# Waiting for each group of four indirect transfers to land before the next group is issued, in a four-layer graph network

## The chip, the cores and the metric

The kernel runs on one core of one Trainium2 chip. The metric is the device time of one execution in microseconds (us), as the median of several runs. The engines are named as the profile names them: PE is TensorE, DVE is VectorE, ACT is ScalarE, POOL is GpSimd, SP is SyncE, which here issues the plain transfers.

## The reference

A graph of 6250 nodes and 100,000 edges, sorted by destination, with 128 features per node, goes through four layers. Each layer adds its result to the input and normalises the rows. Every layer works on rows gathered by edge:

```python
edge_index = jnp.stack([src, dst])
x = _layernorm(x + _L0_gnn_ref(x, edge_index, edge_weight, ...))       # three hops of a weighted sum over edges
x = _layernorm(x + _L1_gnn_ref(x, node_type_8, src, dst, edge_type_8, ...))  # typed attention, softmax over dst
x = _layernorm(x + _L2_gnn_ref(x, edge_index, ...))                    # attention on leaky_relu(x_l[src] + x_r[dst])
x = _layernorm(x + _L3_gnn_ref(x, edge_index, ...))                    # attention, softmax over src, summed over dst

def spmm(z):                                                           # one hop of layer 0
    return jax.ops.segment_sum(edge_weight[:, None] * z[col], row, num_segments=N)
```

## The kernel before

Edges are handled in chunks of 128, one edge per partition, and chunks in groups of four (`G = 4`). There are 784 chunks of edges (`EC`, 196 groups), or 832 (`CH`, 208 groups) where the list is padded so that each chunk touches one block of 128 nodes. Whatever is addressed by an edge's index goes through an indirect transfer that POOL issues: one instruction per chunk, 128 rows each, 7200 of them in all. The stages follow one another:

- `scatter_edges` (issue at L726, 784 transfers): DVE and PE work out the place of every edge in the order by source, and POOL scatters records of four numbers (16 bytes) to these places in HBM. POOL waits for `placed`, once per group.
- `hop`, called three times (issue at L1094, 784 transfers each): POOL gathers rows of 512 bytes into a ring of 16 groups, in `rows`. SP waits for each group's `got` and counts `landed`; PE multiplies the landed rows by weighted one-hot tiles (L1137); DVE makes these tiles (L1171) and adds the sums (L1184). From the 17th group on POOL waits for PE's count `summed` before it issues a group. Beside hops 1 and 2 the places for the order by destination are worked out, beside hop 0 a histogram.
- `scatter_ranked` (issue at L1292, 784 transfers): the scatter into the order by destination. POOL waits for nothing between its transfers. PE, DVE, ACT and SP go on to the dense work of layer 0 meanwhile.
- `softmax_pass`, called three times (issue at L1443; 832, 832 and 784 transfers): rows of 1024, 528 and 512 bytes are gathered for layers 1, 2 and 3. The ring is 11, 15 and 16 groups deep. Before it reuses a slot, POOL waits for DVE's `weighed` or `scored` (L1815, L1752).
- `weigh_and_sum` (issue at L1938, 832 transfers of 1056-byte rows): the change doesn't touch it.

Each group has a completion semaphore per ring slot (`got[s]`, `sent[s]`), raised by 16 by each transfer once it has landed, so 64 per group and turn of the ring. In `scatter_ranked` the four transfers of a group raise four different semaphores. POOL executes its instructions in the order in which they are written; the code isn't reordered by a scheduler.

Of the kernel before, what the change touches and what calls it, by code (L numbers as in the profile page):

```python
# [21 lines left out]
G = 4  # L22
SLOTS = 4
# [21 lines left out]
RING = 16  # L45
# [532 lines left out]
def scatter_edges(nc, k, rec, keys, first_place, table, name):  # L578


    with ExitStack() as ctx:
# [25 lines left out]
        sent = [sem(f"sent{s}") for s in range(SLOTS)]  # L607
# [4 lines left out]
        @block.scalar  # L612
        def _(act):
            def turn_onehots(n, b):

                act.wait_ge(turned_ok, n + 1)
                act.wait_ge(looked, n * G + G)
                nc.scalar.copy(oh_lo_t[:, b, :, :], turned[:, b, 0:G, :]).then_inc(lo_t, 1)

            def a_round(i, first):  # L620
                for s in range(SLOTS):
                    n = i * SLOTS + s
                    if not first:

                        act.wait_ge(sent[s], i * 64)
                    nc.scalar.copy(records[:, s, :, :], rec[:, bass.ds(i * SLOTS * G + s * G, G), :]).then_inc(taken, 1)
                    for g in range(G):
                        if g == G - 1:
                            turn_onehots(n + 1, (s + 1) % 2)

                        act.wait_ge(next_ready, n * G + g + 1)
                        act.wait_ge(looked, n * G + g + 2 * G - 1)
                        nc.scalar.copy(next_sb[:, g % 2, :], next_ps[:, 0:HIS]).then_inc(next_copied, 1)

            turn_onehots(0, 0)
            in_rounds(act, groups // SLOTS, a_round)
# [81 lines left out]
        @block.gpsimd  # L718
        def _(pool):
            with pool.Fori(0, groups // SLOTS) as i:  # L720
                for s in range(SLOTS):

                    pool.wait_ge(placed, i * SLOTS + s + 1)
                    pool.sem_inc(running, 1)
                    for g in range(G):
                        nc.gpsimd.indirect_dma_start(table, bass.IndirectOffsetOnAxis(ap=places[:, s, g:g + 1], axis=0),  # L726
                                                     records[:, s, g, :], None).then_inc(sent[s], 16)
            for s in range(SLOTS):
                pool.wait_ge(sent[s], 64 * (groups // SLOTS))

# [251 lines left out]
def hop(nc, k, o, table_in, table_out, name, tally=None, rank=None, shared=None, listed=None):  # L982
# [3 lines left out]
    with ExitStack() as ctx:  # L986
# [6 lines left out]
        got = [sem(f"got{s}") for s in range(RING)]  # L993
# [89 lines left out]
        def _(pool):  # L1083
            if listed is not None:
                pool.wait_ge(listed, 2)
            for n in range(GU):
# [5 lines left out]
                for g in range(G):  # L1092
# [2 lines left out]
                                                 bass.IndirectOffsetOnAxis(ap=o.gather[:, c:c + 1], axis=0),  # L1095
                                                 ).then_inc(got[s], 16)

        @block.tensor
        def _(pe):
            def rank_columns(r, s, half):  # L1100
                b = s % 2
                if half == 0:

                    pe.wait_ge(lo_t, r + 1)
                    pe.wait_ge(ranked, r + 1)
                for g in range(2 * half, 2 * half + 2):

                    pe.wait_ge(next_copied, r * G + g + 1)
                    nc.tensor.matmul(next_ps[:, 0:HIS], oh_lo[:, s, g, :], oh_hi[:, s, g, :], start=False,  # L1109
                                     stop=False, skip_group_check=True).then_inc(next_ready, 1)  # L1110
                    nc.tensor.matmul(nexts[:, b, g, 0:HIS], oh_lo_t[:, b, g, :], next_sb[:, g % 2, :], start=True,
                                     stop=True).then_inc(looked, 1)
                    if g == 0:

                        pe.wait_ge(taken, r + 1)
                        pe.wait_ge(onehots, r + 2)
                        pe.wait_ge(matched, r + 2)
                        for h in range(G):
                            last = nc.tensor.transpose(keyrow[:, h, :], column[:, b, h:h + 1].to_broadcast([P, P]),
                                                       k.ident[:])  # L1120
                        last.then_inc(rows_ok, 1)
                        for h in range(G):
                            last = nc.tensor.transpose(turned[:, 1 - b, h, :], oh_lo[:, (s + 1) % SLOTS, h, :], k.identb[:])
                        last.then_inc(turned_ok, 1)

            def a_round(i, first, ranks):
                for s in range(DEEP):
                    b = s % 2
                    n = i * DEEP + s
                    slots = load_blocks(nc, pe.engine, o.slot[:, bass.ds(n * G, G)], G, RING * G - 1)  # L1130
                    need = pe.value_load(o.need[:, bass.ds(n, 1)], min_val=1, max_val=GU)
                    pe.wait_ge(landed, need)
                    pe.wait_ge(hot, n + 1)

                    pe.wait_ge(added, (n + 1) * G)
                    for g in range(G):
                        last = nc.tensor.matmul(sums[:, b, g, :], weighted[:, s % SLOTS, g, :],  # L1137
                                                rows[:, bass.ds(slots[g], 1), :], start=True, stop=True)
                    last.then_inc(summed, 1)
                    if tally is not None:  # L1140
                        pe.wait_ge(marked, n + 1)
                        for g in range(G):
                            last = nc.tensor.matmul(tallies[:], tally_hi[:, b, g, :], tally_lo[:, b, g, :], start=False,
                                                    stop=False, skip_group_check=True)
                        last.then_inc(tallied, 1)
                    if ranks:
                        rank_columns(i * (DEEP // 2) + s // 2, s // 2, s % 2)

            pe.sem_inc(summed, SLOTS)
            if tally is not None:  # L1150
                pe.sem_inc(tallied, 2)
                pe.wait_ge(zeroed, 1)
                nc.tensor.matmul(tallies[:], zero[:, 0:HIS], zero[:], start=True, stop=False, skip_group_check=True)
            if rank is not None:
                pe.sem_inc(looked, 2 * G)
                rows_first = (k.ident[:], first_place[:])
                turned_first = (first_place[:], k.ident[0:HIS, 0:HIS])
                nc.tensor.matmul(next_ps[:, 0:HIS], *(rows_first if first_place.shape[0] == P else turned_first), start=True,
                                 stop=False, skip_group_check=True).then_inc(next_ready, 1)
                pe.wait_ge(onehots, 1)  # L1160
                for h in range(G):
                    last = nc.tensor.transpose(turned[:, 0, h, :], oh_lo[:, 0, h, :], k.identb[:])
                last.then_inc(turned_ok, 1)
            all_rounds(pe, a_round)
# [116 lines left out]
def scatter_ranked(nc, k, shared, rec, places, table, name, placed):  # L1281


    sent = [nc.alloc_semaphore(f"{name}_sent{s}") for s in range(SLOTS)]
    k.semaphores.extend(sent)

    @shared.gpsimd
    def _(pool):

        pool.wait_ge(placed, 1)  # L1290
        for c in range(EC):
            nc.gpsimd.indirect_dma_start(table, bass.IndirectOffsetOnAxis(ap=places[:, c:c + 1], axis=0),  # L1292
                                         rec[:, c, :], None).then_inc(sent[c % SLOTS], 16)
        for s in range(SLOTS):
            pool.wait_ge(sent[s], 16 * (EC // SLOTS))


def softmax_pass(nc, k, o, index, table, row, head, values_at, spread, att, peaks, total, reload, loops, wg, name, preload=None,
# [21 lines left out]
    ring = lag + 1 if values_at is not None else RING if ringed else 4  # L1320
    with ExitStack() as ctx:
# [40 lines left out]
        got = [sem(f"got{s}") for s in range(ring)]  # L1362
# [70 lines left out]
        @block.gpsimd  # L1433
        def _(pool):
            for n in range(GU if ringed else GROUPS):
                s = n % ring
                if n >= ring:

                    pool.wait_ge(weighed if at else scored, n - ring + 1 + (NBLK // G if ringed else 0))
                    pool.sem_inc(running, 1)  # L1440
                for g in range(G):
                    c = n * G + g
                    nc.gpsimd.indirect_dma_start(rows[:, s, g, :], None, table,  # L1443
                                                 bass.IndirectOffsetOnAxis(ap=index[:, c:c + 1], axis=0),
                                                 ).then_inc(got[s], 16)

        @block.scalar
        def _(act):
# [1778 lines left out]
```

## Time and profile before

| what | us |
|---|---|
| median of 3 runs | 9746.5 (9740.51 to 9749.61) |
| profiled execution, span from the first to the last instruction | 13177.8 |
| POOL busy in it | 7027.7 (53%) |
| PE busy | 6872.9 (52%) |
| DVE busy | 6549.5 (50%) |
| ACT busy | 2082.2 (16%) |
| share of time in which the DMA engines moved the packets of POOL's queue | 14.5% |

The profiled execution took 3431 us longer than the median of the runs. The profile gives no time for it besides its span. In a row of the timeline the first number is the start, the second the duration; the brackets hold how long the engine had been idle and what released it. "issue" means that nothing shown in the profile was waited for. For POOL the recorded duration of an indirect transfer is that of the instruction that issues it, and the data land later.

### The profile page before, as it was taken

What the parts mean: (1) busy time and instruction counts of PE and PEld (TensorE: products, weight loads), DVE (VectorE), ACT (ScalarE), POOL (GpSimd) and SP (SyncE); (2) the same over time, 40 slices, a digit from 0 to 9 for tenths busy, and PEclk for the clock granted to TensorE, in tenths of its full rate; (3) what the DMA queues carried; (4) which work ended last, traced back from release to release, by engine and by line L of the source; (5) the groups of instructions that cost most, each with busy time, mean ns of one, the idle gap of its engine ahead of it and who ended that gap; (6) DMA issues with size and microseconds to landing.
All of it is one profiled execution on the core that took longest, in us unless ns stands there. A gap on an engine that the chain in (4) does not pass through costs nothing. (4 is left out here: it accounts for less than half of the span.)

```text
span 13177.8 us, 169349 instructions
## 1 busy us (share of the span) xinstructions
PE 6872.9 (52%) x37679; PEld 6012.4 (46%) x37680; DVE 6549.5 (50%) x22663; ACT 2082.2 (16%) x6208; POOL 7027.7 (53%) x7417
## 2 busy tenths in 40 slices
PE   5555444445554555100384555656666566665555
PEld 4444333335554555100234455456665465654444
DVE  6444455555555555200265555755556344455555
ACT  4222100001110111000121111311222111122222
POOL 6555566646664666777205555245553555535554
PEclk6555555556666666555687777877787555556766
DMA  0000011111111111010143222111112211112232
GB/s 19 1 1 1 21 44 44 44 42 42 42 43 40 42 42 43 16 22 8 50 157 79 74 74 74 56 38 39 39 39 65 52 38 38 38 47 77 79 81 74
DMA packets 436083, 614.60 MB, mean 47 GB/s; under 512 B 176625, under 2 KB 312133, under 8 KB 435173
## 3 DMA queue, kind: packets, MB, share of 16 engines
q0 software_dynamic: 257024, 486.93, 14.5%
q1 hardware_dynamic: 178369, 119.49, 3.2%
q8 instruction: 183, 3.00, 0.1%
q10 hardware_dynamic: 292, 3.41, 0.1%
q14 instruction: 215, 1.76, 0.0%
HBM read 520.17 MB, written 89.19 MB: 46 GB/s over the span
## 5 line engine op out<-in xcount | busy, mean ns | idle before, releaser
L1094 POOL DMA_INDIRECT hop_rows<-hops,k_src_gather x1568 | 1479.3, 943 | 1077.3 <-issue 435.9
L1137 PE MATMUL hop_sums<-hop_rows,hop_weighted 128*128 x4992 | 1159.9, 405 | 1110.7 <-DVE k_x L1184 736.1
L1137 PEld LDWEIGHTS hop_sums<-hop_rows,hop_weighted 128*128 128x128 f32 x4992 | 1009.7, 300 | 1201.7 <-issue 1200.4
L1443 POOL DMA_INDIRECT l_pass_rows<-related,k_dst_typed x832 | 786.2, 945 | 1216.8 <-POOLq L74 517.6
L1443 POOL DMA_INDIRECT l_pass_rows<-left_table,k_dst_other x832 | 786.6, 945 | 895.7 <-DVE l_pass_terms L1815 490.5
L1938 POOL DMA_INDIRECT l_weigh_rows<-row_table,l_weigh_ring x832 | 813.0, 977 | 733.8 <-ACT l_weigh_ring L1902 466.3
L1443 POOL DMA_INDIRECT l_pass_rows<-key_table,k_src_gather x784 | 739.5, 943 | 766.6 <-DVE l_pass_scores L1752 387.3
L726 POOL DMA_INDIRECT src_sorted<-src_scatter_records,src_scatter_places x784 | 750.6, 957 | 606.3 <-DVE src_scatter_places L714 393.6
L1538 PE MATMUL l_pass_sums<-l_pass_zero 128*128 128x272 bf16 (+1 forms) x1210 | 262.7, 306 | 1454.0 <-DVE l_total L1632 1005.2
L1094 POOL DMA_INDIRECT hop_rows<-in_x,k_src_gather x784 | 739.6, 943 | 456.4 <-issue 220.8
L1292 POOL DMA_INDIRECT dst_sorted<-rec,dst_places x784 | 809.2, 1032 | 262.1 <-issue 262.1
L1171 DVE TENSOR_SCALAR hop_weighted<-k_numbers,k_src_place,src_weight 128x128 f32<-128x128 f32 x2496 | 861.1, 404 | 136.7 <-issue 125.4
L1459 ACT CAST l_pass_onehot_t<-l_pass_turned 128x512 f32<-128x512 bf16 x624 | 365.1, 585 | 3006.3 <-remote 960.0
L1538 PEld LDWEIGHTS l_pass_sums<-l_pass_zero 128*128 128x128 bf16 x1210 | 109.3, 116 | 1544.3 <-DVE l_total L1632 1052.2
L1956 PE MATMUL l_weigh_own<-l_keys,l_weigh_onehot_t 128*128 x1672 | 367.2, 388 | 689.4 <-ACT l_weigh_onehot_t L1908 604.0
L1109 PE MATMUL hop_next_ps<-hop_oh_hi,hop_oh_lo 128*128 128x50 bf16 x784 | 180.9, 231 | 919.4 <-ACT hop_next_sb L1072 787.3
L1956 PEld LDWEIGHTS l_weigh_own<-l_keys,l_weigh_onehot_t 128*128 128x128 f32 x1672 | 313.5, 280 | 733.9 <-issue 733.9
L1548 PE MATMUL l_pass_sums<-l_pass_terms,l_pass_onehot_f 128*128 128x136 f32 x3232 | 625.8, 355 | 1.1 <-DVE l_pass_terms L1815 1.1
L1548 PEld LDWEIGHTS l_pass_sums<-l_pass_terms,l_pass_onehot_f 128*128 128x128 f32 x3232 | 585.2, 261 | 28.2 <-issue 3.3
L1109 PEld LDWEIGHTS hop_next_ps<-hop_oh_hi,hop_oh_lo 128*128 128x128 bf16 x784 | 97.9, 125 | 982.9 <-ACT hop_next_sb L1072 821.4
L1072 ACT COPY hop_next_sb<-hop_next_ps 128x50 f32<-128x50 f32 x784 | 158.5, 202 | 2192.7 <-remote 725.2
L662 PE MATMUL src_scatter_nexts<-src_scatter_next_sb,src_scatter_oh_lo_t 128*128 128x50 f32 x1568 | 493.5, 425 | 0.0
(467 smaller groups left out, 18342.8 us busy)
## 6 DMA issues: line engine op xcount, KB each, us to landing
related<-l_tables_rows SPq DMA_DIRECT2D x50, 1024.0 KB, 4.4
hop_rows<-hops,k_src_gather POOLq DMA_INDIRECT x1568
l_pass_rows<-related,k_dst_typed POOLq DMA_INDIRECT x832
l_pass_rows<-left_table,k_dst_other POOLq DMA_INDIRECT x832
l_weigh_rows<-row_table,l_weigh_ring POOLq DMA_INDIRECT x832
src_sorted<-src_scatter_records,src_scatter_places POOLq DMA_INDIRECT x784
hop_rows<-in_x,k_src_gather POOLq DMA_INDIRECT x784
dst_sorted<-rec,dst_places POOLq DMA_INDIRECT x784
```

The costliest lines, as they stand in the source:

```text
L662: nc.tensor.matmul(nexts[:, b, g, 0:HIS], oh_lo_t[:, b, g, :], next_sb[:, g % 2, :], start=True, stop=True).then_inc(looked, 1)
L726: nc.gpsimd.indirect_dma_start(table, bass.IndirectOffsetOnAxis(ap=places[:, s, g:g + 1], axis=0), records[:, s, g, :], None).then_inc(sen ...
L1094: nc.gpsimd.indirect_dma_start(rows[:, s * G + g, :], None, table_in, bass.IndirectOffsetOnAxis(ap=o.gather[:, c:c + 1], axis=0),).then_in ...
L1137: last = nc.tensor.matmul(sums[:, b, g, :], weighted[:, s % SLOTS, g, :], rows[:, bass.ds(slots[g], 1), :], start=True, stop=True)
L1171: last = nc.vector.tensor_scalar(weighted[:, s, g, :], k.numbers, o.place[:, c], o.weight[:, c], ALU.is_equal, ALU.mult)
L1292: nc.gpsimd.indirect_dma_start(table, bass.IndirectOffsetOnAxis(ap=places[:, c:c + 1], axis=0), rec[:, c, :], None).then_inc(sent[c % SLOT ...
L1443: nc.gpsimd.indirect_dma_start(rows[:, s, g, :], None, table, bass.IndirectOffsetOnAxis(ap=index[:, c:c + 1], axis=0),).then_inc(got[s], 16)
L1459: nc.scalar.copy(onehot_t[:, n % 2, :, :], turned[:, 0:G, :]).then_inc(copied, 1)
L1538: nc.tensor.matmul(into[:, 2 * half:2 * half + 2, 0:width], zero[:, 0:P], zero[:, 0:2 * width], start=True, stop=False, skip_group_check=True)
L1548: last = nc.tensor.matmul(into[:, bass.ds(within[g], 1), 0:width], onehot_f[:, m % 2, g, :], term, start=False, stop=False, skip_group_che ...
L1938: nc.gpsimd.indirect_dma_start(rows[:, s, g, :], None, table, bass.IndirectOffsetOnAxis(ap=ring[:, s, g:g + 1], axis=0),).then_inc(got[s], 16)
L1956: last = nc.tensor.matmul(own[:, b, g, :], onehot_t[:, b, g, :], spread[:, bass.ds(blocks[g], 1), :], start=True, stop=True)
```

## The change

POOL gets one more wait after each fourth indirect transfer, on the completion semaphore of what it has just issued, in four of the five functions that issue them.

```diff
@@ scatter_edges (L726)
                     for g in range(G):
                         nc.gpsimd.indirect_dma_start(table, bass.IndirectOffsetOnAxis(ap=places[:, s, g:g + 1], axis=0),
                                                      records[:, s, g, :], None).then_inc(sent[s], 16)
+
+                    pool.wait_ge(sent[s], i * 64 + 64)
@@ hop (L1094)
                                                  bass.IndirectOffsetOnAxis(ap=o.gather[:, c:c + 1], axis=0),
                                                  ).then_inc(got[s], 16)
 
+                pool.wait_ge(got[s], (n // RING + 1) * 16 * G)
@@ scatter_ranked (L1292)
         for c in range(EC):
             nc.gpsimd.indirect_dma_start(table, bass.IndirectOffsetOnAxis(ap=places[:, c:c + 1], axis=0),
                                          rec[:, c, :], None).then_inc(sent[c % SLOTS], 16)
+            if c % SLOTS == SLOTS - 1:
+
+                pool.wait_ge(sent[SLOTS - 1], 16 * (c // SLOTS + 1))
@@ softmax_pass (L1443)
                                                  bass.IndirectOffsetOnAxis(ap=index[:, c:c + 1], axis=0),
                                                  ).then_inc(got[s], 16)
 
+                pool.wait_ge(got[s], (n // ring + 1) * 16 * G)
```

On POOL, the first hop's issue reads as follows before; `src_read_listed` says that the list of rows is there, and `hop0_summed` is PE's count.

```order
L1094 DMA hop_rows<-in_x,k_src_gather 128x128 [waits src_read_listed]
L1094 DMA hop_rows<-in_x,k_src_gather 128x128 x63
L1094 DMA hop_rows<-in_x,k_src_gather 128x128 [waits hop0_summed]
L1094 DMA hop_rows<-in_x,k_src_gather 128x128 x3
L1094 DMA hop_rows<-in_x,k_src_gather 128x128 [waits hop0_summed]
```

The same place on POOL with the change, from the start of the hop; `hop0_got0` to `hop0_got15` are the completion semaphores of the ring's slots.

```order
L1096 DMA hop_rows<-in_x,k_src_gather 128x128 [waits src_read_listed]
L1096 DMA hop_rows<-in_x,k_src_gather 128x128 x3
L1096 DMA hop_rows<-in_x,k_src_gather 128x128 [waits hop0_got0]
L1096 DMA hop_rows<-in_x,k_src_gather 128x128 x3
L1096 DMA hop_rows<-in_x,k_src_gather 128x128 [waits hop0_got1]
L1096 DMA hop_rows<-in_x,k_src_gather 128x128 x3
...
L1096 DMA hop_rows<-in_x,k_src_gather 128x128 [waits hop0_got15,hop0_summed]
L1096 DMA hop_rows<-in_x,k_src_gather 128x128 x3
```

No transfer has changed its place. Each group's first transfer now waits for the group before it, in the later groups besides PE's count; the first 64 transfers had no wait among them. In the scatter by source, whose body of four groups is a loop on POOL, the piece of the difference is this; `src_scatter_placed` is DVE's count of placed groups, `src_scatter_sent0` the completion of the group just issued.

```order
 L726 DMA src_sorted<-src_scatter_records,src_scatter_places 106881x4 [waits src_scatter_placed]
 L726 DMA src_sorted<-src_scatter_records,src_scatter_places 106881x4 x3
-L723 REGISTER_ALU
+L723 REGISTER_ALU [waits src_scatter_sent0]
 L726 DMA src_sorted<-src_scatter_records,src_scatter_places 106881x4 [waits src_scatter_placed]
 L726 DMA src_sorted<-src_scatter_records,src_scatter_places 106881x4 x3
```

There too the order is as before, and the register instruction between two groups carries the wait.

## Rows read from the trace of the kernel before

**Rows 1.** The page's head and its first part.
```profile
span 13177.8 us, 169349 instructions
PE 6872.9 (52%) x37679; PEld 6012.4 (46%) x37680; DVE 6549.5 (50%) x22663; ACT 2082.2 (16%) x6208; POOL 7027.7 (53%) x7417
```

**Rows 2.** Instructions by source line on POOL: duration ns min/median/max, first and last start.
```profile
L726 POOL DMA_INDIRECT src_sorted<-src_scatter_records,src_scatter_places x784: 952/958/1201, 160.7 to 1494.6; - x196
L1094 POOL DMA_INDIRECT hop_rows<-in_x,k_src_gather x784: 938/944/982, 1511.5 to 2697.1; - x196
L1094 POOL DMA_INDIRECT hop_rows<-hops,k_src_gather x1568: 938/944/1358, 2755.3 to 5310.8; - x196
L1292 POOL DMA_INDIRECT dst_sorted<-rec,dst_places x784: 954/959/2607, 5312.1 to 6382.0; - x196
L1443 POOL DMA_INDIRECT l_pass_rows<-related,k_dst_typed x832: 940/946/987, 6900.7 to 8385.2; - x167
L1443 POOL DMA_INDIRECT l_pass_rows<-left_table,k_dst_other x832: 938/944/2175, 8566.2 to 10067.5; - x167
L1443 POOL DMA_INDIRECT l_pass_rows<-key_table,k_src_gather x784: 938/944/959, 10202.1 to 11573.7; - x196
L1938 POOL DMA_INDIRECT l_weigh_rows<-row_table,l_weigh_ring x832: 940/946/1389, 11693.4 to 13120.0; - x167
```

**Rows 3.** Waits of POOL: us in total, times, longest us.
```profile
POOL l_pass_rows L1443 <- DVE l_pass_terms L1815: 955.0, 271, 63.9
...
POOL l_pass_rows L1443 <- POOLq L74: 517.6, 1, 517.6
...
POOL src_sorted L726 <- DVE src_scatter_places L714: 393.6, 115, 22.0
POOL l_pass_rows L1443 <- DVE l_pass_scores L1752: 387.3, 81, 42.5
POOL hop_rows L1094 <- remote: 374.9, 131, 3.8
```

**Rows 4.** Timeline of POOL in the scatter by destination.
```profile
5400.46 0.96 POOL L1292 DMA_INDIRECT dst_sorted<-rec,dst_places  x1 [0.30 <-issue]
```

**Rows 5.** Timeline of PE at the end of hop 0, POOL issuing nothing.
```profile
2703.19 2.07 PE L1137 MATMUL hop_sums<-hop_rows,hop_weighted 128*128 x8 [0.37 <-DVE k_x L1184]
2706.18 2.07 PE L1137 MATMUL hop_sums<-hop_rows,hop_weighted 128*128 x8 [0.36 <-DVE k_x L1184]
```

**Rows 6.** Timeline of PE at the end of hop 2, POOL in the scatter by destination.
```profile
5349.66 2.07 PE L1137 MATMUL hop_sums<-hop_rows,hop_weighted 128*128 x8 [19.63 <-issue]
...
5370.66 2.07 PE L1137 MATMUL hop_sums<-hop_rows,hop_weighted 128*128 x8 [18.93 <-DVE k_x L1184]
```

**Rows 7.** Timeline of SP's queue in layer 0's dense work.
```profile
5675.38 761.00 SPq L2177 DMA_DIRECT2D poly_z<-hops  x30
...
6878.33 0.81 SPq L763 DMA_DIRECT2D dst_read_lst<-dst_sorted  x2
```

**Rows 8.** Windows: length, busy PE, PEld, DVE, ACT, POOL, PEclk, DMA share, GB/s.
```profile
1495.60:1496.40 0.80, 0.00 (x0) 0.00 (x0) 0.00 (x0) 0.00 (x0) 0.00 (x1) 0.50 0.04 3
1496.40:1499.00 2.60, 0.00 (x0) 0.00 (x0) 0.00 (x0) 0.00 (x0) 0.00 (x0) 0.50 0.00 0
...
2698.70:2699.40 0.70, 0.00 (x0) 0.00 (x0) 0.00 (x0) 0.00 (x0) 0.00 (x0) 0.50 0.34 94
2699.40:2703.00 3.60, 2.63 (x12) 2.16 (x12) 3.23 (x12) 0.00 (x0) 0.00 (x0) 0.50 0.00 0
```

**Rows 9.** Timeline at the start of layer 2's pass, POOL and PE.
```profile
8569.98 1.47 POOL L1443 DMA_INDIRECT l_pass_rows<-left_table,k_dst_other  x1 [0.30 <-issue]
...
8573.43 0.79 PE L1520 MATMUL l_pass_own<-l_right,l_pass_onehot_t 128*128 x2 [3.85 <-DMA l_pass_rows<-left_table,k_dst_other]
```

**Rows 10.** Timeline of DVE and POOL in the scatter by source.
```profile
731.55 0.16 DVE L714 TENSOR_TENSOR src_scatter_places<-src_scatter_base,src_scatter_earlier 128x4 int32<-128x4 f32 x1 [0.24 <-DVE src_scatter_picked L705]
...
732.50 0.95 POOL L726 DMA_INDIRECT src_sorted<-src_scatter_records,src_scatter_places  x1 [4.49 <-DVE src_scatter_places L714]
```

## The prediction, made before the changed kernel was run

> **What bounds the kernel now.** I read the page's head first, because span and runs differ: the profiled execution took 13177.8 us [rows 1], the median of the runs is 9746.5. The 3431 us between them must be placed before anything is summed. PE, DVE and POOL are all busy for about half of the span [rows 1], so shares name no bound. POOL's indirect transfers, by line, come next [rows 2]: 784 + 784 + 1568 + 784 + 832 + 832 + 784 + 832 = 7200, each 0.944 to 0.959 us of POOL in the median whatever it moves. The timeline shows 0.30 us between two that follow each other without a wait [rows 4]. So POOL needs 0.944 + 0.30 = 1.245 us per transfer, 4.98 per group of four, and 7200 x 1.245 = 8964 us in all.
>
> What lies outside these stages is the span less the eight stretches from first to last start [rows 2]: 1333.9 + 1185.6 + 2555.5 + 1069.9 + 1484.5 + 1501.3 + 1371.6 + 1426.6 = 11928.9, and 13177.8 - 11928.9 = 1249. In this trace POOL doesn't run at its floor. It waits for its consumers, 955.0 + 387.3 us in the passes, 393.6 in the scatter by source, 374.9 in the hops [rows 3].
>
> Are these waits in the timed runs as well? The end of a hop tells. With POOL silent PE takes a group each 2.99 us [rows 5]; with POOL in its unbroken row of scatters the same work takes 21.0 us a group, nearly all of it idle [rows 6]. So in this trace the other engines crawl while POOL issues. The dense work of layer 0 does too: its 30 loads are spread over 761 us, nearly all of them beside the scatter that ends at 6383 [rows 7, 2]. It is this that makes POOL wait 517.6 us for the block's end [rows 3].
>
> Now take the crawl away. Hop 2's tail would be 12 groups of 2.99 = 36 us, the dense work about 700 us in all (the 495 us left at 6383 up to the read at 6878 [rows 7], and some 200 before), which fits under the 976 us that 784 scatters need at 1.245. Behind the scatter only the read of the list would remain, from 6878.3 to 6900.7 [rows 7, 2], 22 us in place of 517.6. Outside the stages that leaves 1249 - 496 = 753. The sum is 8964 + 753 = 9717, 0.3% under the median of the runs. I take this as the strongest reading here: the timed runs are bound by POOL's issue from end to end, and POOL's waits and the crawl belong mostly to the profiled execution.
>
> **The change, part by part.** Nothing is removed or moved. What is added is a wait behind each fourth transfer: 196 groups in each scatter, 3 x 196 = 588 in the hops, 208 + 208 + 196 = 612 in the passes, so 392 scatter groups and 1200 gather groups, 1592 waits. The 208 groups of the last stage keep their form. Queued behind each wait is the next group's first transfer, on POOL alone; no other engine's order changes. SP, PE and DVE wait for the landings of the same group, which come as late after its issue as before, but the next group is issued later.
>
> The price of a wait is (landing after POOL's fourth instruction has ended) + (POOL's restart) - (the 0.30 us that pass anyway).
>
> Landing of a gather: hop 0's last issue ends at 2697.1 + 0.94 = 2698.1. The DMA engines still move 94 GB/s x 0.70 us = 66 KB, one transfer, up to 2699.4, and nothing after [rows 8]. So the lower bound is 1.24 us, for 64 KB. The upper bound is PE's start in layer 2's pass: the fourth issue ends at 8571.45, PE begins at 8573.43 [rows 9], 1.98 us later, its own restart included. Landing of a scatter of 2 KB: the last issue ends at 1494.64 + 0.96 = 1495.6, and the traffic is over by 1496.4 [rows 8]: 0.8 us.
>
> Restart: DVE has the places at 731.71, POOL starts its transfer at 732.50 [rows 10], 0.79 us later.
>
> From end to next start a gather group thus takes at least 1.24 + 0.79 = 2.03 us and at most 1.98 + 0.79 = 2.77. I take 2.1, near the lower end, since the upper one counts a restart twice. For a scatter I take 0.8 + 0.79 and a little for the semaphore, 1.8. Less 0.30 the terms are 1.8 and 1.5 us:
>
> - scatter by source: 196 x 1.5 = 294. DVE's chain runs ahead of POOL, so nothing hides it.
> - hops: 588 x 1.8 = 1058. The consumers take 3 us a group [rows 5] where POOL will take 4.98 + 1.8 = 6.8.
> - scatter by destination: 196 x 1.5 = 294. The cover would be the dense work, but by the sum above that is the shorter side, 700 against 976 us, so the term counts in full. Were the dense work as slow as in this trace, up to 496 us of slack would take all of it.
> - passes: 612 x 1.8 = 1102. Wider rows (1024 bytes) may land some tenths later.
>
> Sum: 294 + 1058 + 294 + 1102 = 2748 us. Against the median that is 9746.5 + 2748 = 12,495 us, 28% slower. Against the profiled execution the same sum would give 13177.8 + 2748 = 15,926 if nothing were hidden there; but there POOL already waits for crawling engines, and the new waits take the place of part of that, so I expect its span to rise by far less, to 13,200 to 14,500.
>
> By the rows a gather is bounded between 1.24 and 1.98 us after the issue. The Trainium skill, "DMA: Bandwidth & Descriptors", section "Anatomy of one DMA", gives for a transfer from this queue about 2.0 us plus its bytes over 436 GB/s, so 2.15 us for 64 KB counted from the issue, 1.21 behind POOL's 0.94. By it the gather term would be 1.21 + 0.79 - 0.30 = 1.70 and the sum some 120 us smaller; it speaks for the lower end of the rows' range.
>
> **The rivals.**
>
> *Short wait.* Landing at the end of the traffic, and POOL restarts with no more than the usual 0.30: 1.24 x 1200 + 0.8 x 392 = 1802, so 11,550 us. For it: nothing shows a restart without the recording of the trace. Against it: the 0.79 [rows 10].
>
> *Long wait.* 2.77 - 0.30 = 2.47 x 1200 + 1.5 x 392 = 3552, so 13,300 us. For it: PE's start [rows 9]. Against it: it counts two restarts.
>
> *Waits already there.* POOL's waits of the trace are real, and the new ones lie inside. Each stage then keeps the longer of its pace in the trace and POOL's new floor of 6.8 us a group (6.5 for scatters). The paces are 6.81, 6.05, 6.5 twice, 5.46, 7.14, 7.22 and 7.00 [rows 2], so only the hops and the scatter by destination grow: 196 x 0.73 + 392 x 0.3 + 196 x 1.5 = 555, so 10,300 us. Against it: the sum to 9717 leaves no room for such waits.
>
> *Faster: the pauses free the other engines.* The place is the stretch from 5312 to 6901. If the crawl of rows 6 is in the timed runs too, a POOL that falls silent for some 2 us per group lets the others through. Layer 0's dense work then ends beside the scatter, and the stretch shrinks from 1589 us to the scatter's 1070 + 294 and the read's 22, a gain of 203; in hops and passes the new waits replace the old. That gives 9,545 us. It decides if more than a third of POOL's time in the timed runs were such waits. For it: rows 5 against rows 6, a factor of seven. Against it: the same sum.
> The Trainium skill, "SBUF — State Buffer", states that VectorE's operations in some modes lock GpSimd out of writing descriptors. Pauses would not shorten that; L1292's longest instruction, 2.607 us against 0.959 in the median [rows 2], may be such a case, and they are too few to change the sum.
>
> *No effect.* The group has landed before POOL reaches the wait. The last traffic begins after the issue has ended [rows 8], which all but excludes it.
>
> **How the numbers follow.** Forecast 0.64, short wait 0.15, long wait 0.05, waits already there 0.09, faster 0.05, no effect 0.02. The range reaches down to the short wait and up to 13,000: 11,500 to 13,000 holds 0.64, nearly all of the short case and part of the long, about 0.8. A change of 0.2% (20 us) can just be told from none. Faster by more than that: 0.05; within it: 0.02; slower: 0.93.
>
> **What would show it.** In the new trace POOL should be idle some 2.1 us before each group's first transfer in hops and passes and 1.8 in the scatters, released by the transfers; the durations of 0.944 and 0.959 and the 0.30 inside a group should stay. The scatter by destination should take 1070 + 294 = 1364 us, and the dense work beside it should crawl less. The stage at L1938 should stay near 1427 us. The forecast is wrong if the time lies under 11,000 (the waits were hidden, and the timed runs aren't bound by POOL), and a term is mis-sized if POOL's idle time between groups differs from 2.1 us.

## The result, and the profile after

The changed kernel takes 12,987.4 us in the median of 3 runs (12,968.6 to 12,994.0), the kernel before 9746.5. The ratio is 1.332, interval 1.330 to 1.334: 3241 us slower, or 2.04 us for each of the 1592 added waits. On most chips the kernel before takes 9725 to 9750 us, but on two chips used later it took 13,164 to 13,204 us in every run; its trace shown above has a span of that second kind, while the ratio belongs to chips of the first. Its second profiled execution, `e_before_again` below, was on a chip of the first kind, and the trace after is compared with that one.

POOL's transfers by line in that second trace of the kernel before: duration ns min/median/max, first and last start.

```profile
L726 POOL DMA_INDIRECT src_sorted<-src_scatter_records,src_scatter_places x784: 954/958/1203, 160.1 to 1148.9; - x196
...
L1094 POOL DMA_INDIRECT hop_rows<-hops,k_src_gather x1568: 940/944/1361, 2165.0 to 4141.8; - x196
L1094 POOL DMA_INDIRECT hop_rows<-in_x,k_src_gather x784: 940/944/977, 1165.4 to 2142.9; - x196
...
L1292 POOL DMA_INDIRECT dst_sorted<-rec,dst_places x784: 954/958/4121, 4143.0 to 5148.6; - x196
...
L1443 POOL DMA_INDIRECT l_pass_rows<-related,k_dst_typed x832: 940/946/982, 5174.8 to 6237.9; - x167
L1443 POOL DMA_INDIRECT l_pass_rows<-left_table,k_dst_other x832: 940/944/7362, 6417.8 to 7470.4; - x167
L1443 POOL DMA_INDIRECT l_pass_rows<-key_table,k_src_gather x784: 940/944/1344, 7603.7 to 8584.9; - x196
...
L1938 POOL DMA_INDIRECT l_weigh_rows<-row_table,l_weigh_ring x832: 942/946/1151, 8632.9 to 9672.1; - x167
```

The same lines of the changed kernel, which answer to [rows 2].

```profile
L726 POOL DMA_INDIRECT src_sorted<-src_scatter_records,src_scatter_places x784: 955/962/1204, 160.2 to 1503.5; - x196
...
L1096 POOL DMA_INDIRECT hop_rows<-hops,k_src_gather x1568: 941/947/1651, 2926.9 to 5722.1; - x196
L1096 POOL DMA_INDIRECT hop_rows<-in_x,k_src_gather x784: 939/947/978, 1520.7 to 2904.6; - x196
...
L1296 POOL DMA_INDIRECT dst_sorted<-rec,dst_places x784: 953/962/3975, 5725.6 to 7009.8; - x196
...
L1450 POOL DMA_INDIRECT l_pass_rows<-related,k_dst_typed x832: 941/949/985, 7036.5 to 8621.0; - x167
L1450 POOL DMA_INDIRECT l_pass_rows<-left_table,k_dst_other x832: 939/947/6996, 8796.2 to 10289.8; - x167
L1450 POOL DMA_INDIRECT l_pass_rows<-key_table,k_src_gather x784: 941/947/1385, 10425.3 to 11843.4; - x196
...
L1947 POOL DMA_INDIRECT l_weigh_rows<-row_table,l_weigh_ring x832: 942/949/1022, 11888.8 to 12930.3; - x167
```

From first to last start the stages compare like this. The last column is the difference over the number of waits, so an average.

| stage | before | after | difference | per wait |
|---|---|---|---|---|
| scatter by source | 988.8 | 1343.3 | 354.5 | 1.81 |
| hop 0 | 977.5 | 1383.9 | 406.4 | 2.07 |
| hops 1 and 2 | 1976.8 | 2795.2 | 818.4 | 2.09 |
| scatter by destination | 1005.6 | 1284.2 | 278.6 | 1.42 |
| pass of layer 1 | 1063.1 | 1584.5 | 521.4 | 2.51 |
| pass of layer 2 | 1052.6 | 1493.6 | 441.0 | 2.12 |
| pass of layer 3 | 981.2 | 1418.1 | 436.9 | 2.23 |
| last stage, without added waits | 1039.2 | 1041.5 | 2.3 | |

The differences sum to 3259 us; the spans, 9728.6 and 12985.7, differ by 3257. Nearly all of the loss lies between POOL's transfers: the transfers themselves have kept their durations to 0.004 us in the median. What POOL waits for in the trace after (us in total, times, longest) answers to [rows 3]:

```profile
POOL hop_rows L1096 <- DMA hop_rows<-hops,k_src_gather: 909.6, 387, 3.4
...
POOL l_pass_rows L1450 <- DMA l_pass_rows<-related,k_dst_typed: 592.8, 206, 13.1
POOL l_pass_rows L1450 <- DMA l_pass_rows<-key_table,k_src_gather: 484.3, 193, 11.5
POOL l_pass_rows L1450 <- DMA l_pass_rows<-left_table,k_dst_other: 455.9, 189, 4.6
POOL hop_rows L1096 <- DMA hop_rows<-in_x,k_src_gather: 451.1, 193, 3.1
POOL dst_sorted L1296 <- DMA dst_sorted<-rec,dst_places: 340.1, 195, 19.8
```

The releaser is the transfer just issued, once per group. The waits for DVE that led the list in the first trace, 955.0 and 387.3 us, are 42.0 us in all here; that isn't the work of the change, since on this kind of chip they were only 57.5 us without it, in `e_before_again`. One group boundary of each kind, from POOL's timeline after: early in hop 0, in hop 1, in layer 1's pass, in the scatter by destination, and there once more, the longest.

```profile
1527.21 0.94 POOL L1096 DMA_INDIRECT hop_rows<-in_x,k_src_gather  x1 [1.80 <-DMA hop_rows<-in_x,k_src_gather]
...
3504.28 0.95 POOL L1096 DMA_INDIRECT hop_rows<-hops,k_src_gather  x1 [2.37 <-DMA hop_rows<-hops,k_src_gather]
...
7799.22 0.94 POOL L1450 DMA_INDIRECT l_pass_rows<-related,k_dst_typed  x1 [2.67 <-DMA l_pass_rows<-related,k_dst_typed]
...
6801.73 0.96 POOL L1296 DMA_INDIRECT dst_sorted<-rec,dst_places  x1 [1.43 <-DMA dst_sorted<-rec,dst_places]
...
5790.94 0.96 POOL L1296 DMA_INDIRECT dst_sorted<-rec,dst_places  x1 [19.79 <-DMA dst_sorted<-rec,dst_places]
```

The price isn't one number. It is smallest for 2 KB scatters and largest for 1024-byte rows, and within a hop POOL is idle 1.80 us before each of the first groups and 2.37 behind the 16th; the price is this less the 0.30 that passed before.

An average can hold two things. In the scatter by destination the usual group costs 1.43 - 0.30 = 1.13 us, and the average is 1.42 because some landings come late: 21 of the 195 idle times are over 1.7 us, all of them between 5736 and 6319, while SP's transfers for the dense work run (5729 to 6322), and together they take 54 us more than usual. Layer 1's pass has idle times of up to 13.1 us at its start. Without the waits such a late landing didn't hold POOL up: in the same scatter of `e_before_again` it is never idle for more than 0.3 us.

The profile page's part on transfers gives the landing itself, as median us from issue to landing:

```profile
src_sorted<-src_scatter_records,src_scatter_places POOLq DMA_INDIRECT x784, 2.1
hop_rows<-in_x,k_src_gather POOLq DMA_INDIRECT x784, 2.5
dst_sorted<-rec,dst_places POOLq DMA_INDIRECT x784, 2.1
```

Less the instruction's own 0.94 and 0.96 us, a gather of 64 KB has landed 1.56 us after it and a scatter 1.14. So 1.80 is a landing and 0.24 of restart, 1.43 a landing and 0.29; but 2.37 is a landing and 0.81. The record of the completion semaphore in hop 0 says the same: in the median it is full 1.56 us after the fourth instruction has ended, and 0.32 after the last packet of POOL's queue. For 1024-byte rows POOL's queue goes on 1.82 us after the fourth instruction.

### The profile page after: what moved, and what is told of

Read it like the earlier page. It is cut to its first block and busy times, and to the rows that moved or that the text cites. A ratio compares the mean times of both kernels' runs of the same rounds, so it can differ in the third digit from the quotient of the medians.

```text
span 12985.7 us, 169404 instructions
## 1 busy us (share of the span) xinstructions
PE 7036.1 (54%) x37679; PEld 6148.6 (47%) x37680; DVE 6554.1 (50%) x22663; ACT 2125.4 (16%) x6208; POOL 6982.5 (54%) x7417
## 5 line engine op out<-in xcount | busy, mean ns | idle before, releaser
L1141 PE MATMUL hop_sums<-hop_rows,hop_weighted 128*128 x4992 | 1242.0, 427 | 2146.1 <-SPq L1277 1672.9
L1141 PEld LDWEIGHTS hop_sums<-hop_rows,hop_weighted 128*128 128x128 f32 x4992 | 1067.6, 316 | 2258.0 <-issue 2257.7
L1296 POOL DMA_INDIRECT dst_sorted<-rec,dst_places x784 | 764.7, 975 | 523.1 <-DMA dst_sorted<-rec,dst_places 340.1
L1529 PE MATMUL l_pass_own<-l_right,l_pass_onehot_t 128*128 x1664 | 449.1, 363 | 501.0 <-DMA l_pass_rows<-left_table,k_dst_other 488.9
L1529 PEld LDWEIGHTS l_pass_own<-l_right,l_pass_onehot_t 128*128 128x128 f32 x1664 | 347.7, 259 | 537.2 <-issue 537.2
L1204 DVE SCALAR_TENSOR_TENSOR hop_same<-hop_keyrow,hop_column,k_before 128x128 f32<-128x128 f32 x784 | 228.1, 347 | 571.1 <-PE hop_keyrow L1123 571.0
L1730 DVE TENSOR_TENSOR l_pass_pair<-l_pass_own,l_pass_rows 128x128 f32<-128x128 f32 x832 | 184.5, 283 | 652.7 <-SPq L1431 608.8
L660 PE MATMUL src_scatter_next_ps<-src_scatter_oh_hi,src_scatter_oh_lo 128*128 128x50 bf16 x784 | 179.7, 229 | 593.4 <-ACT src_scatter_next_sb L633 593.4
```

The lines of the kernel that those rows point to most:

```text
L1204: last = nc.vector.scalar_tensor_tensor(out=same[:, g, :], in0=keyrow[:, g, :], scalar=column[:, b, g:g + 1], in1=k.before[:], op0=ALU.is_ ...
L1529: last = nc.tensor.matmul(own[:, b, g, :], onehot_t[:, b, g, :], spread[:, bass.ds(blocks[g], 1), :], start=True, stop=(att is None))
```

## The experiments

**The kernel before again.** `e_before_again`: nothing is edited.

> The kernel before, unchanged, for a second profiled execution. If POOL's waits for its consumers and the crawl of the other engines come from recording the trace while POOL issues without a pause, the profiled span is again near 13,180 us with the time near 9,746 us. If they belonged to that one execution only, the span is near 9,750. If they are in the timed runs, the time would have to be near the span, which it wasn't.

It took 9730.5 us with a span of 9728.6. The span of 13,178 is therefore not made by recording a trace as such. Within a hop POOL is never idle but for the 0.30 us between two transfers (704.1 us in 2311 gaps, the longest 0.3); in the passes it is so nearly everywhere. POOL's waits, us in total, times, longest:

```profile
POOL l_pass_rows L1443 <- issue: 707.7, 2306, 1.4
POOL hop_rows L1094 <- issue: 704.1, 2311, 0.3
...
POOL dst_sorted L1292 <- issue: 239.0, 784, 0.3
```

This shows what the prediction had worked out as a sum: on this kind of chip POOL's issue bounds every gathering and scattering stage.

**One part alone.** Three kernels carry the waits of one function each.

`e_hops`, in `hop` alone:
```diff
+                pool.wait_ge(got[s], (n // RING + 1) * 16 * G)
```

> Only the waits in the three hops, 588. If POOL's issue bounds the timed runs and each wait adds what POOL stands idle in the trace after (2.35 us on average instead of 0.30, so 2.04), the time is 9746 + 588 x 2.04 = 10,950 us. If part of a wait is hidden behind slack that the other stages' waits use up too, it is well below, nearer 10,300 us.

Measured 10,956.1 us, ratio 1.1255 (1.1236 to 1.1274): 1217 us more than the 9738.9 of the kernel before on that chip, 2.07 per wait.

`e_scatter2`, in `scatter_ranked` alone:
```diff
+            if c % SLOTS == SLOTS - 1:
+                pool.wait_ge(sent[SLOTS - 1], 16 * (c // SLOTS + 1))
```

> Only the waits in the scatter by destination, 196. POOL bound, with the dense work of layer 0 the shorter side: 196 x 1.44 = 282 us, so 10,030 us. If the dense work covers the scatter in the timed runs as it did in the trace of before (517.6 us of slack), nothing: 9,746 us.

Measured 10,016.2 us, ratio 1.0283 (1.0266 to 1.0300): 277 us, nothing hidden. The dense work beside it is the shorter side. In the trace of the changed kernel SP has stored its last result of that work at 6322 and reads the sorted list only at 7014, behind the scatter:

```profile
5814.86 66.91 SPq L2186 DMA_DIRECT2D poly_z<-hops  x30
...
6322.32 0.41 SPq L943 DMA_DIRECT2D src_breaks<-src_breaks_end  x1
7013.68 0.82 SPq L765 DMA_DIRECT2D dst_read_lst<-dst_sorted  x2
```

`e_passes`, in `softmax_pass` alone:
```diff
+                pool.wait_ge(got[s], (n // ring + 1) * 16 * G)
```

> Only the waits in the three softmax passes, 612. POOL bound: 208 x 2.57 + 208 x 2.11 + 196 x 2.20 = 1,405 us, so 11,150 us. If the passes' consumers bound the timed runs before (POOL waited 1342 us for them in the trace of before), little: 9,800 to 10,300 us.

Measured 11,123.6 us, ratio 1.1423 (1.1404 to 1.1443): 1385 us. The three parts give 1217 + 277 + 1385 = 2879; the scatter by source, not run alone, has 354.5 in the table; together 3234 of 3241 us. The parts add up, so no slack is shared between them.

**The same waits, one group later.** `e_one_behind`: POOL waits for the group before the one it has just issued. The edit in `hop` is shown; the passes have the same, the scatter by source has it at three of four groups, and the scatter by destination has it with eight completion semaphores in place of four.

```diff
-                pool.wait_ge(got[s], (n // RING + 1) * 16 * G)
+                if n >= 1:
+                    pool.wait_ge(got[(n - 1) % RING], ((n - 1) // RING + 1) * 16 * G)
```

> As many waits as in the change, but each is on the group before the one just issued (in the scatter by source three of four; the scatter by destination has eight completion semaphores in place of four for it). If the price is the exposed landing and restart, it goes to nothing, since a group has landed long before the next one's fourth transfer is issued (1.24 against 4.98 us): 9,740 to 9,800 us. If executing a wait and what follows it costs the restart of 0.7 to 1.1 us each time, the time is 10,800 to 11,300 us.

Measured 9770.2 us, ratio 1.0037 (1.0023 to 1.0051): 35 us for some 1540 waits. POOL's waits in hops and passes:

```profile
POOL l_pass_rows L1451 <- issue: 722.4, 2303, 1.6
POOL hop_rows L1097 <- issue: 680.1, 2232, 0.3
```

A wait that is met when POOL comes to it costs nothing that shows: from first to last start the hops take 977.4 and 1976.6 us and the scatter by source 988.7, within 0.2 us of `e_before_again`. The 35 us lie elsewhere, where single landings come late enough to outlast a group: the scatter by destination takes 1020.3 us instead of 1005.6, with one idle time of 14.9 us. So the price of the change is the exposed landing and what can't be prepared before it.

**Half as many.** `e_every_second`: the waits stand at every second group, in all four functions (the scatter by destination again with eight semaphores).

```diff
+                if n % 2 == 1:
+                    pool.wait_ge(got[s], (n // RING + 1) * 16 * G)
```

> The waits of the change at every second group only, 796 in place of 1592. Price per wait constant: half of the 3,241 us, so 11,370 us. If POOL catches up in the group without a wait, because the consumers set the pace, less: 10,000 to 10,800 us.

Measured 11,415.2 us, ratio 1.1726 (1.1707 to 1.1746): 1680 us, 2.11 per wait. POOL doesn't catch up in the group without a wait: there it is idle for 0.30 us, as everywhere before.

**The increment behind the wait.** `e_no_running`: the changed kernel without POOL's `running` in hops and passes.

```diff
                     pool.wait_ge(summed, n - RING + 2 + NBLK // G + SLOTS)
-                    pool.sem_inc(running, 1)
```

> The changed kernel without POOL's increment of the semaphore running (nothing waits for it) in hops and passes. In the trace after, POOL is idle 1.85 us between the first 16 groups of a hop and 2.37 in the later ones, which have this increment and the wait for the consumer besides. If the increment makes that difference, 540 + 570 = 1110 groups save 0.52 us, 577 us: 12,410 us. If it is the second wait, nothing: 12,987 us.

Measured 12,323.8 us, ratio 1.2648 (1.2627 to 1.2669) to the kernel before, 664 us less than the changed kernel's time above and 641 less than its time in `e_after_again`. A group boundary in hop 1:

```profile
3508.07 0.94 POOL L1095 DMA_INDIRECT hop_rows<-hops,k_src_gather  x1 [1.79 <-DMA hop_rows<-hops,k_src_gather]
```

So 2.37 becomes 1.79, the idle time of the first groups, though the wait for `summed` is still there. The increment makes the difference, 664 / 1110 = 0.60 us each; by 641 us, or by the stretches of the five stages alone, which are 644 us shorter, it is 0.58. In the changed kernel's trace the increment's own instruction carries the wait for the landing, and the next transfer starts 0.80 us after it. Here the transfer itself carries the wait and starts 0.26 us after the landing. Another instruction in that place was not tried, so this doesn't tell whether the increment alone costs that much.

**The increment without the wait.** `e_before_no_running` and `e_before_no_running_2` are one kernel, the kernel before with the same edit.

> The kernel before without POOL's increment of the semaphore running in hops and passes. Behind the wait for a landing its removal saved 664 us. Without that wait POOL's queue executes it while the fourth transfer is still being issued, if the reasons given hold, so nothing: 9,735 us within 0.2%. If the increment costs its 0.5 to 0.6 us by itself, 1110 x 0.6 = 664 us less: 9,070 us, faster than both kernels.

> The kernel before without POOL's increment of the semaphore running in hops and passes, again, since the first time it ran on a chip on which the kernel before itself took 13,197 us and the increment's removal gave 167 us. On a chip where the kernel before takes 9,735 us: the same within 0.2% if POOL's queue hides the increment, 9,070 us if it costs 0.6 us each time. On a chip of the other kind again some 13,030 us.

The first ran on a chip on which the kernel before took 13,197.1 us: 13,030.0 us, ratio 0.9877 (0.9861 to 0.9894). The second ran on a chip of the usual kind: 9731.7 beside 9732.2 us, ratio 1.0001 (0.9991 to 1.0010). There the increment is free, and it costs about 0.6 us once a wait for the landing stands before it. The reason expected for this, that POOL's queue executes it under a transfer that is still being issued, is not what the trace shows: in the hops of `e_before_again` 507 of the 540 increments stand in the gap between two transfers, most of them 0.02 us behind the one and 0.28 before the next, which starts no later for it. Why the same instruction is followed by 0.80 us after a real wait stays open, and so does where the 167 us of the first run come from.

**The stage that was left out.** `e_weigh`: the kernel before with the wait in `weigh_and_sum` alone.

```diff
                     for g in range(G):
                         nc.gpsimd.indirect_dma_start(rows[:, s, g, :], None, table, ...).then_inc(got[s], 16)
+                    pool.wait_ge(got[s], i * 64 + 64)
```

> The kernel before with the wait in the one stage that the change leaves out, the 208 groups of weigh_and_sum. Landing 1.46 us as for the 1024-byte rows of layer 1, and 1.23 us until POOL starts, as in the scatter by source, whose wait also stands in a loop before a register's value: (2.69 - 0.30) x 208 = 497 us, so 10,240 us. If its chain over four slots is closer to its limit than POOL's issue shows, the loop gets slower on top: above 10,400 us.

Measured 10,246.9 us, ratio 1.0526 (1.0508 to 1.0543): 512 us for 208 waits, 2.46 each. A group boundary of it:

```profile
9000.39 0.95 POOL L1938 DMA_INDIRECT l_weigh_rows<-row_table,l_weigh_ring  x1 [2.68 <-DMA l_weigh_rows<-row_table,l_weigh_ring]
```

The price taken from other stages by row size and form of loop held to 3%, though not by its parts. The increment, which comes 0.08 us behind the wait, stands 1.93 us after the end of the fourth instruction and 0.75 us before the next transfer, where 1.46 and 1.23 had been expected; two errors cancelled.

**The changed kernel on either kind of chip.** `e_after_again` and `e_after_fourth` are the changed kernel, unedited.

> The changed kernel once more, beside the kernel before on the same chip. One chip ran the kernel before at 13,197 us in seven runs, as the first trace of it did, another at 9,735. On a chip of the second kind: 12,980 us, ratio 1.33. On a chip of the first kind the other engines crawl while POOL issues, and POOL's new pauses are of the length of its waits there, about 1.7 to 2.2 us per group: hops and passes stay at their pace, the last stage with no added wait keeps its 1428 us where it took 1042, so 13,200 to 13,500 us, ratio 1.00 to 1.02. If the crawl doesn't care for POOL's pauses, the 3,241 us come on top: 16,400 us.

> The changed kernel a third time, for the chance of a chip of the kind on which the kernel before takes 13,197 us. There: 13,200 to 13,500 us, ratio 1.00 to 1.02, if the pauses let the other engines through; 16,400 us if the crawl doesn't care for them. On the other kind: 12,970 us, ratio 1.33, as twice before.

The first met a chip with the kernel before at 9732.2 us: 12,964.8, ratio 1.3321 (1.3299 to 1.3343). The second met one with the kernel before at 13,187.8 us: 13,361.6, ratio 1.013 (1.0113 to 1.0147), inside what was expected for that case. The same change costs 3233 us on the one kind and 174 on the other. On the second kind POOL still waits for its own transfers alone in the hops, as on the first; SP's loads of layer 0 take 73 us instead of 761 [rows 7], and 67 on the first kind; only the last stage, without added waits, is slow:

```profile
5807.65 72.95 SPq L2186 DMA_DIRECT2D poly_z<-hops  x30
```

```profile
POOL hop_rows L1096 <- DMA hop_rows<-hops,k_src_gather: 910.6, 387, 3.1
...
POOL l_weigh_rows L1947 <- ACT l_weigh_ring L1911: 439.6, 103, 44.5
```

```profile
L1947 POOL DMA_INDIRECT l_weigh_rows<-row_table,l_weigh_ring x832: 940/946/1386, 11867.1 to 13318.0; - x167
```

That stage takes 1450.9 us where it took 1041.5, a difference of 409; the spans differ by 391. With its pauses in, POOL lets the other engines through, and the rest of the kernel runs alike on both kinds of chip.

## Why the prediction came out as it did

The direction, the mechanism and the place were right: POOL's issue bounds the runs, and each wait lays a landing open. The size was too small. The time, 12,987.4 us, lies inside the range, but 0.1% below its upper end, and that is luck: the forecast of 12,495 was 492 us too low, and the measured time is nearer to the long wait, 13,300, which had been given 0.05. The mean price of a gather wait was 2.19 us, against 1.8 in the forecast and 2.47 in the long wait. Of the missing time the passes make some 300 us, the hops 167 and the scatter by source 61. By its steps:

- *The timed runs have POOL at its floor, 7200 x 1.245 us, though its trace shows 13,178 us.* Right. The sum of 9717 us is met by a span of 9728.6, the 22 us of the read by 26 (5148.6 to 5174.8), the dense work "about 700" by 597 in the changed kernel (from 5725.6, the scatter's first start, to 6322.3, where SP stores its last result).
- *The crawl belongs mostly to the profiled execution.* Right in that the timed runs shown didn't have it, wrong about its cause. It goes with the chip that a run meets, and is found in timed runs too. On which chip the first trace was taken is not on record; that its span, 13,178, fits the second kind is an inference.
- *No slack hides anything, the scatter by destination included.* Right: the parts add up to within 7 us.
- *Scatter by destination, 1.5 us a wait.* Measured 1.42, but this agreement is chance. The usual price is 1.13, a landing of 1.14 and a restart of 0.29 in place of the 0.79 assumed; late landings beside the dense work make up the rest.
- *Hops, 1.8.* Measured 2.08. The mis-sized term is the landing. From PE's start and the end of the traffic [rows 8, 9] I had taken 1.3 us for the landing. It is 1.56: the semaphore follows the last packet by 0.32 us. The restart of 0.79 [rows 10] held, at 0.81, but only where the increment stands behind the wait; in a hop's first 16 groups it is 0.24. The estimate worked out from the Trainium skill, "DMA: Bandwidth & Descriptors", section "Anatomy of one DMA", 1.21 us behind the instruction, is lower still; this trace doesn't agree with it, by 0.35 us.
- *Scatter by source, 1.5.* Measured 1.81. Its loop has the wait for `placed` and the increment behind the new wait, as the hops have, and a register instruction besides: POOL starts 0.86 us after a landing of 1.13, in the median, so the usual price is 1.99 - 0.30 = 1.69. The landing had been taken as 0.8 and a little.
- *Passes, 1.8, "wider rows may land some tenths later".* Measured 2.51, 2.12 and 2.23. This is the largest part of the miss. The median idle times are 2.62, 2.40 and 2.36 us, so the usual prices 2.32, 2.10 and 2.06: the same landing and restart as in the hops, and for rows of 1024 bytes some 0.26 more of landing, which had been written down and not put into the sum. What the averages have above that is for the most part late landings, up to 13.1 us of idle time in the first pass and 11.5 in the third.
- With the measured prices the sum is 196 x 1.81 + 588 x 2.08 + 196 x 1.42 + 208 x (2.51 + 2.12) + 196 x 2.23 = 3256 us, against 3241.
- *The profiled span rises to between 13,200 and 14,500.* Wrong as written: 12,985.7, since that execution was on a chip without the crawl. On a chip with it the span is 13,376.9.
- The rival by which pauses free the other engines was given 0.05 for the timed runs. It is what happens on the other kind of chip, where the change costs 3233 - 174 = 3059 us less, yet it isn't enough to make the kernel faster.

What stays open: why two of the chips let the other engines crawl while POOL issues without a pause. The runs show that it goes with the chip and that pauses of about 2 us per four transfers end it; they don't show whose resource it is, and since each of the two chips was met only once, not whether it is lasting. Of the other kernels only the one before without the increment ran on such a chip. On the usual chips none of the variants is faster than the kernel before; one group behind, the wait is harmless.

## What to carry to other kernels

Before a profiled span is used, set it beside the timed runs; where they differ by a third, work out from the issuing engine's floor (its transfers times the time between two starts) which of its waits the timed runs can have room for. A wait for a landing on the engine that issues the transfers costs the landing plus the engine's restart, about 2 us here, once per wait, when that engine is the bound; the same wait one group later costs almost nothing, 35 us for some 1540 of them. It also exposes the engine to every landing that other traffic makes late. What is queued behind such a wait may be paid too, as the unused semaphore increment was here. And an average price per wait can agree with a sum whose parts are wrong; set the idle time of single groups beside it.

## What the runs showed of the hardware that was not expected

- Two kinds of chip: the kernel before takes 9725 to 9750 us on the one and 13,164 to 13,204 on the other, within 0.3% each. In the trace of the second kind PE takes 21.0 us for a group that takes 2.99 when POOL is silent [rows 5, 6].
- POOL's semaphore increment costs nothing between transfers that follow each other without a wait (9731.7 against 9732.2 us) and about 0.6 us behind a wait for a landing.
- The completion of a 64 KB gather arrives 1.56 us after the issuing instruction has ended, 0.32 us behind its last packet; that of a 2 KB scatter after 1.14. Beside SP's transfers of the dense work single scatters landed so late that POOL stood idle for up to 19.8 us.
